# Sandwich layer on eight cores: eight weight slots and a reordered start for the first unit, scratch copies kept by five units

## The reference

```python
# x: (32, 2048, 1024) f32
x = x + layernorm(attn(layernorm(x)))
x = x + layernorm(ffn(layernorm(x)))

def attn(x):       # 16 heads of 64; segments of 512 tokens, every 4th token belongs to a head's set
    Q, K, V = x @ Wq + bq, x @ Wk + bk, x @ Wv + bv
    # head h takes, in each segment, the tokens with offset h % 4 (128 of them)
    scores = sum(Qs * Ks, over the 64 elements) * 64 ** -0.5
    attn = softmax(scores, over the 128 tokens)[..., None] * Vs
    # zero elsewhere
    return out @ Wo + bo

def ffn(x):        # integer weights, int32, times 1/127
    h = silu(x @ wg.T) * (x @ wu.T)      # hidden 3072
    return h @ wd.T
```

## Time and profile before

| | us |
|---|---|
| median of 3 runs | 2325.8 (2325.51 to 2326.94) |
| the profiled execution | 2324.59 |
| its span, slowest core | 2323.0 (the other cores 2317.4 to 2322.8) |
| PE busy | 2232.1 (96%) |
| DVE, ACT, POOL busy | 987.4, 645.4, 233.5 |
| mean granted clock of PE | 0.99 |

### The profile page before, as it was taken

One profiled execution on the slowest core, in us unless ns is written; L12 is line 12 of the kernel. 1 busy time (PEld: TensorE's weight loads), 2 busy tenths in 40 slices (PEclk: granted clock), 3 DMA queues, 4 the chain that ended last, 5 costly groups with the idle time before them and its releaser, 6 DMA issues.

```text
span 2323.0 us, 31558 instructions; the slowest of 8 cores (2317.4 to 2323.0 us)
## 1 busy us (share of the span) xinstructions
PE 2232.1 (96%) x10193; PEld 1017.1 (44%) x10400; DVE 987.4 (43%) x1697; ACT 645.4 (28%) x848; POOL 233.5 (10%) x633
## 2 busy tenths in 40 slices
PE   4789989999999999999999999999999999999997
PEld 2334434444444444444444444444444444444443
DVE  3552352534525344352544525344362544435222
ACT  3313213232231322313232231322323232231311
POOL 4211111010100101001010100101001010100100
PEclk9899999999999999999999999999999999999999
DMA  9696876764435444455544445355543534434340
GB/s 197 104 172 150 166 188 129 215 137 151 145 110 183 107 148 129 139 157 134 180 105 155 134 124 171 96 171 139 151 145 109 173 109 155 127 118 145 90 146 37
DMA packets 201953, 327.74 MB, mean 141 GB/s; under 512 B 127936, under 2 KB 127936, under 8 KB 201792
## 3 DMA queue, kind: packets, MB, share of 16 engines
q1 hardware_dynamic: 70272, 255.88, 34.0%
q0 software_dynamic: 12672, 39.85, 10.9%
q10 hardware_dynamic: 118848, 29.98, 7.1%
HBM read 290.01 MB, written 46.14 MB: 145 GB/s over the span
## 4 chain that ended last, share of the span: by engine, by line
PE 90%; DMA 6%; issue 1%; ACT 1%; ACTq 1%; DVE 1%; SPq 0%; POOL 0%; POOLq 0%; DVEq 0%
PE pf L479 27%; PE pf L475 27%; PE pf L493 26%; PE pa L401 7%; PE pa L450 2%; DMA gu<-wgu 2%; DMA x<-x 2%; DMA scr_gu<-gu 1%; ACTq L775 1%; ACT xh L752 0%; DMA xT<-xh 0%; PE pt L395 0%; PE pf L401 0%; PE pa L438 0%; DMA gu<-scr_gu 0%
## 5 line engine op out<-in xcount | busy, mean ns | idle before, releaser
L475 PE MATMUL pf<-xT,gu 128*128 128x512 bf16 x3010 | 724.8, 381 | 21.9 <-DMA gu<-wgu 12.6
L479 PE MATMUL pf<-xT,gu 128*128 128x512 bf16 x3012 | 722.4, 380 | 3.3 <-issue 0.2
L493 PE MATMUL pf<-wd_sb,h 128*128 128x512 bf16 x3009 | 662.8, 379 | 3.3
L632 DVE TENSOR_TENSOR h<-silu,pf 128x512 bf16<-128x512 bf16 x384 | 264.0, 687 | 795.8 <-PE pf L479 642.9
L802 ACT ACTIVATE silu<-pf 128x512 bf16<-128x512 f32 x384 | 228.8, 596 | 973.9 <-PE pf L475 950.4
L475 PEld LDWEIGHTS pf<-xT,gu 128*128 128x128 bf16 x3072 | 300.9, 98 | 385.6 <-issue 27.7
L479 PEld LDWEIGHTS pf<-xT,gu 128*128 128x128 bf16 x3072 | 301.6, 98 | 365.6 <-issue 5.7
L493 PEld LDWEIGHTS pf<-wd_sb,h 128*128 128x128 bf16 x3072 | 300.3, 98 | 361.6
L281 POOL TENSOR_SCALAR stats<-stats 128x1 f32<-128x1 f32 (+1 forms) x124 | 29.9, 241 | 1829.6 <-DVE stats L563 1825.7
L642 DVE TENSOR_TENSOR x<-y,x 128x1024 f32<-128x1024 f32 x64 | 78.3, 1223 | 301.1 <-ACT y L815 301.1
L401 PE MATMUL pa<-xT,wqkv_sb 128*128 128x512 bf16 x722 | 167.0, 383 | 6.3 <-DMA xT<-xh 2.3
(11 more groups left out here) (43 smaller groups left out, 685.2 us busy)
## 6 DMA issues: line engine op xcount, KB each, us to landing
gu<-scr_gu SPq DMA_DIRECT2D x336, 512.0 KB, 3.6
x<-x SPq DMA_DIRECT2D x64, 512.0 KB, 5.8
out<-x SPq DMA_DIRECT2D x64, 512.0 KB, 2.7
gu<-wgu POOLq DMA_DIRECT2D x48, 512.0 KB, 9.2
scr_gu<-gu SPq DMA_DIRECT2D x24, 512.0 KB, 8.7
wqkv_sb<-wqkv POOLq DMA_DIRECT2D x12, 512.0 KB, 11.6
wd_sb<-wd POOLq DMA_DIRECT2D x24, 256.0 KB, 30.3
wo_sb<-wo POOLq DMA_DIRECT2D x4, 512.0 KB, 16.0
```

Source lines behind the costliest of these rows:

```text
L475: ins = eng.matmul(g[:], gu[:, o:o + 128], half(xT3, kc), start=(kc == 0), stop=(kc == KC - 1))
L479: ins = eng.matmul(u[:], gu[:, o:o + 128], half(xT3, kc), start=(kc == 0), stop=(kc == KC - 1))
L493: ins = eng.matmul(pf[m % 4][:], h[:, 512 * kc + 128 * j:512 * kc + 128 * j + 128], wd[:, D * kc + 512 * hf:D * kc + 512 * hf + 512], star ...
L632: eng.tensor_mul(half(h, k), half(silu, k % 2), pf[2 * (k % 2) + 1][:]).then_inc(v_h, 1)
```

## The change

Five things are changed.

1. The first unit has a ring of eight slots. Four more (`gux`) lie where the third x buffer `x[2]` lies, which unit 2 is the first to use. From unit 1 on there are four again (`slot`, `gu_slot`, `before`).
2. At the start x of unit 0 is loaded alone. The projection weights wait for its third row and are issued between the rows' `l1` steps, unit 1's x waits for the query weights, and the twelve first down loads come after the gate/up loads. Stores of unit 0's chunks wait until 18 chunks are done; unit 2's x waits for the end of unit 0's gate/up stage and for the last four stores.
3. DVE, ACT and PE have another order in the first unit: unit 1's `ln1` rows stand between the attention steps of unit 0, q of both halves comes before k, `out_proj(0)` before unit 1's transposes, and some `x3_apply` and evictions are swapped. In the tail of unit 0, `ln4(0, 0)` and `fin(0, 0)` stand before the `ln1` rows of unit 2.
4. PE waits for the identity alone, and ACT loads its table with a small exponential ahead of the first row.
5. `kept(k)` spreads the stores: unit 0 keeps 16 to 23, unit 1 keeps 0, 5, 10, 15, unit 2 keeps 1, 6, 11, 12, unit 3 keeps 2, 7, 8, 13, and unit 4 keeps 3, 4, 9, 14. A chunk is cast in each unit up to the one that keeps it: 24, 16, 12, 8 and 4 casting loads instead of 24, 16 and 8.

```diff
-        x = [E(nc.sbuf_tensor(f"x{i}", [128, 4 * D], F32)) for i in range(3)]
+        x = [E(nc.sbuf_tensor(f"x{i}", [128, 4 * D], F32)) for i in range(2)]
+        with contextlib.ExitStack() as pctx:
+            gux = pctx.enter_context(nc.sbuf_tensor("gux", [128, RING * 2 * D], BF16))
+        with contextlib.ExitStack() as pctx:
+            x.append(pctx.enter_context(nc.sbuf_tensor("x2", [128, 4 * D], F32)))
...
+        def kept(k):
+            return 0 if k >= 16 else 1 + (k - k // 4) % 4
         def cast(n):
-            return n % HCN < HCN - 8 * (n // HCN)
+            return n // HCN <= kept(n % HCN)
         def keeps(n):
-            return cast(n) and n % HCN >= HCN - 8 * (n // HCN + 1)
+            return n // HCN == kept(n % HCN)
+        def slot(n):
+            return n % (2 * RING) if n < HCN else n % RING
...
# SP
-                for u in range(2):
+                for j in range(4):
+                    load_x(0, j)
+                if units > 1:
+                    eng.wait_ge(d_q[0], 16)
                     for j in range(4):
-                        load_x(u, j)
+                        load_x(1, j)
+                eng.wait_ge(t_gu, 18)
                 for k in range(16, HCN):
-                    if k == 20 and units > 2:
-                        for j in range(4):
-                            load_x(2, j)
-                    keep_gu(0, k)
+                    keep_gu(k)
+                if units > 2:
+                    eng.wait_ge(t_gu, HCN)
+                    for j in range(4):
+                        eng.wait_ge(d_st[RING + j], 16)
+                        load_x(2, j)
...
# POOL
-                load_attn(0)
-                for k in range(RING):
-                    load_gu(0, k)
                 eng.wait_ge(v_one, 1)
-                for j in range(4):
-                    l1(0, j, 1)
-                    load_wd(2 * j)
-                    load_wd(2 * j + 1)
+                l1(0, 0, 1)
+                eng.wait_ge(d_x[0][2], 16)
+                for j in range(3):
+                    load_proj(0, j)
+                    l1(0, j + 1, 1)
+                load_wo(0)
+                for k in range(2 * RING):
+                    load_gu(k)
                 if units > 1:
                     for j in range(4):
                         l1(1, j, 1)
-                        for k in range(8 + 3 * j, 11 + 3 * j):
-                            load_wd(k)
+                for k in range(12):
+                    load_wd(k)
...
-                for k in range(RING, HCN):
-                    load_gu(0, k)
-                    if k == 15 and units > 1:
+                for k in range(2 * RING, HCN):
+                    load_gu(k)
+                    if k >= 12:
+                        load_wd(k)
+                    if k == 19 and units > 1:
                         l2(1, 0, 4)
-                    if k in (14, 16, 18, 20):
-                        load_wd(13 + k // 2)
...
# ACT
+                eng.wait_ge(v_one, 1)
+                eng.activation(st(IDLE, 4), st(HALF, 4), AF.Exp)
...
                     q_evict(1, 0)
                     q_evict(1, 1)
+                x3_apply(0, 0)
+                if units > 1:
                     v_evict(1, 0)
+                x3_apply(0, 1)
+                if units > 1:
                     v_evict(1, 1)
-                for j in range(4):
-                    x3_apply(0, j)
-                    turn_evict(0, 1, j)
+                turn_evict(0, 1, 0)
+                turn_evict(0, 1, 1)
+                x3_apply(0, 2)
+                turn_evict(0, 1, 2)
+                x3_apply(0, 3)
+                turn_evict(0, 1, 3)
```

More of the change, by code:

```diff
@@ L187, in landed, with scratch @@
         def landed(n):
-            return sum(1 for m in range(n % RING, n + 1, RING) if cast(m) == cast(n))
+            return sum(1 for m in range(n + 1) if slot(m) == slot(n) and cast(m) == cast(n))
         def stores(n):
-            return sum(1 for m in range(n % RING, n + 1, RING) if keeps(m))
+            return sum(1 for m in range(n + 1) if slot(m) == slot(n) and keeps(m))
+        def scratch(n):
+            m = HCN * kept(n % HCN) + n % HCN
+            return d_st[slot(m)], 16 * stores(m)
         def xh_slot(j):
@@ L508, in _ @@
                 proj_v(0, 1)
+                for j in range(4):
+                    out_proj(0, j)
                 if units > 1:
@@ L724, in _ @@
                             ln1(a + 1, j)
-                    for j in range(3):
+                    for j in range(0 if p else 1, 3):
                         ln4(p, j)
@@ L840, in _ @@
                 if units > 1:
[L841 to L842 removed]
+                    for j in range(4):
+                        x1_apply(1, j)
                     for j in range(4):
```

119 lines of the change are left out of this document (64 added, 55 removed).

## The result

The changed kernel takes 2299.6 us (median of three runs, 2298.4 to 2301.6) where the kernel before takes 2326.0 us (median of four): the ratio is 0.9887, with a 95% interval of 0.9868 to 0.9907. Forecast were 2295.0 us in a range of 2284 to 2309, so the direction was right, and the gain of 26.4 us is 3.2 us (a ninth) smaller than the 29.6 us of the sum. In a later session the same kernel took 2299.4 us.

What follows compares the result with a forecast made beforehand. The kernel was taken as bound by matmuls wherever they are fed, so only PE's losses could be won. Terms -8.9 - 11.8 - 0.5 - 9.4 + 1.0 = -29.6 us, from 2324.6 to 2295.0 us; range 2284 to 2309.

Steps and rivals of the forecast that it cites:

- x alone and first: Start: x of unit 0 lands sooner with casting loads behind it; projections start at 22.2 us, -6.0 us.
- Unit 1's rows between unit 0's vector work: Start, on DVE: each row holds back only what comes after it; output projection at 46.0 instead of 55.74 us.
- The check that I named, the scores waiting for over 3 us: Start: forecast wrong there if the scores still wait for a unit 1 row by more than 3 us.
- Output projection before the transposes: Start, on PE: output projection ahead of unit 1's transposes; first gate matmul at 78.0 us, -8.9 us, ends 74 and 83.
- rival 1: Start bound by delivery: x no faster, unit 1's rows at 47 us, first gate matmul at 83; 2300 us, chance 0.12.
- Eight slots, stores held back: Unit 0's gate/up stage: no load waits for a store; 88.7 us, -11.8 us, ends 87 and 96.
- The sign that I named, no wait for gate/up weights in unit 0: Unit 0's gate/up stage: PE never waits for gate/up weights, stage under 90 us.
- Down of unit 0: Unit 0's down stage: scaled rows ready since POOL no longer stands in loads waiting for stores; -0.5 us.
- Scratch kept by five units: Unit 1's gate/up stage: fewer stores, 3 us lost instead of 12.4, -9.4 us; units 2 to 4 cast more, +1.0 us.
- Rival 2: Feed stays short: unit 0 keeps 7 us of stalls, unit 1 keeps 9 us; 2308 us, chance 0.15.
- Rival 3: Units 2 to 4: 18 casting loads each miss by 3.6 us, losing 65 us; 2359 us, chance 0.03.
- Rival 4: All goes well: POOL's issues hide, unit 1 loses nothing, first gate matmul at 74; 2286 us, chance 0.08.

Runs made afterwards that it cites:

- stores not held back: The changed kernel without the wait that holds unit 0's stores until 18 chunks are done; 2307.8 us, ratio 0.9907 to the kernel before.
- x not alone: The changed kernel with all loads at the start asked for together as before, unit 1's x right behind unit 0's; 2302.0 us, ratio 0.9905 to the kernel before.
- rows late: The changed kernel with unit 1's four statistics later on DVE and four down loads between POOL's `l1` steps; 2297.8 us, ratio 0.9867 to the kernel before.

## Why the prediction was right, and where it was off

- **x alone and first** (-6.0 for the projections): -5.1 from slowest core to slowest core (28.16 to 23.06), -4.8 on the medians. POOL was last, as said: its three weight issues start at 11.28, 14.07 and 16.70 us. The x queue alone was faster than my 251 GB/s on this core (below), which changed nothing. The price of 2.0 us plus bytes over 436 GB/s, which I held against the trace, is given in the Trainium skill ("DMA: Bandwidth & Descriptors", section on the anatomy of one DMA) for transfers that GpSimd issues. Here x goes by SP's queue, so the trace does not speak against that price.
- **Unit 1's rows between unit 0's vector work** (output projection at 46.0): this is the step that failed; it came at 50.30. The term had the first row 2.0 + 5.4 us after its request. Requested at 18.1 us, it was taken at 29.93: 11.8 us instead of 7.4, and the third at 41.10 instead of 36.7. Between those two the rows took 4.8 and 6.4 us, near my 5.4, so the term that was too small is the first landing among casting loads just issued. The same step has a second mistake: I let each row "hold back only what comes after it" and then costed only the fourth one, while the third stood before a softmax half whose scores were ready. The check that I named, the scores waiting for over 3 us, looked at the wrong place: they waited 2.6 us at most, while the delay came one step later, at the third row before the second softmax half.
- **Output projection before the transposes** (first gate at 78.0): the step itself held. From the output projection's start to the first gate matmul I had 32.0 us, measured are 32.5 (50.30 to 82.81). Taken back, it costs 4.0 us. The late start was passed on in full, 4.3 us. This is rival 1's number on this core (83), and its time of 2300 us is nearer to the measured 2299.6 than the forecast's 2295.0. Of its mechanism one half came true, unit 1's rows as late as 47 us (46.19); the other, that x of unit 0 gets no faster, did not.
- **Eight slots, stores held back** (-11.8): -12.05, and 90.09 us on the slowest core for the 88.7 forecast. That the term came out so close is in part luck: the hold-back that I took for free carries 5.75 us of it, which the sum does not have. (By my own figures the room was 24.8 us, 166.7 less 2.9 less 139, not 22.) The sign that I named, no wait for gate/up weights in unit 0, held but for one wait: PE stood 0.7 us for a `gux` load on core 2.
- **Down of unit 0** (-0.5): 0. It was core 0's alone; the other cores had 43.2 us before and have it now. Unit 2's x is asked for at 177.65 us (forecast 172 to 183), and costs nothing.
- **Scratch kept by five units** (-9.4 and +1.0): -7.85 and +0.15. The stage takes 99.93 us (100.1 forecast), with 2.2 us of waits on core 2, one of them the named scratch load of chunk 16. The gain is smaller since core 0's 109.52 us was 2.6 us over the median of the cores. DMA's share from 271 to 291 us fell from 1.04 to 0.84.
- **Rival 2** (2308 us): not here, but "stores not held back" is this rival's mechanism, with 2307.8 us on a chip where the kernel before takes 2329.3. **Rival 3** (casting loads late in units 2 to 4): unit 2 takes 97.12 us. **Rival 4** (2286 us): it needed the rows early and unit 1 free of loss; with the rows moved and ACT reordered 2294 us were reached, and unit 1 still lost 2.2 us.

Against the medians of the cores the sum misses by 2.4 us at the start and 1.55 us in unit 1, both less gain than forecast, and the rest nearly cancels. In unit 1 the miss comes with the core the term was read on, the slowest before, whose stage was 2.6 us over the median of the cores. In the start it is the late rows; single cores differ there by 4 us.

Left open: what of unit 1's last 2 us goes when the store leaves the scratch loads' way, why unit 1 takes 2 us more in "x not alone" and "rows late", and the small stalls of unit 3 (0.3 us on the slowest core, up to 0.6 on others). A fifth slot was not tried.

## What to carry to other kernels

On an engine that works in order, ask of each instruction that waits for data of the next unit what stands behind it, and do so for every one of them, not for the last alone: moving four such steps out of the softmax brought the first gate matmul 3.1 us forward here, and 2.4 us more once a few steps of the engines behind were moved too. The same holds for a queue: a store that waited for a casting load held up the load behind it for 5 us, with the DMA engines nearly idle for 3 of them. A transfer that nobody needs yet still takes its share of the DMA engines; one wait that held eight stores back was worth 5.75 us, and work moved into a stage that is short of transfers cost 10.3 us with few slots. Before a faster delivery is built, look whether its consumers can take it: at the first gate matmul x alone was worth nothing in one order and 4.5 us in the other.

## What the runs showed of the hardware

From 6 to 10 us, where only x of unit 0 moves, and then from 40 to 70 us, where casting loads fill the engines; and the 16 matmuls of the output projection in the changed kernel, and 15 of them in the kernel before:

```profile
6.00:10.00 4.00, 0.00 (x0) 0.00 (x0) 2.03 (x4) 0.00 (x0) 1.15 (x4) 1.00 0.97 303
40.00:70.00 30.00, 17.62 (x86) 7.89 (x86) 25.20 (x49) 12.28 (x13) 16.93 (x37) 0.77 1.05 177
50.30:55.75 5.45, 5.45 (x19) 2.13 (x20) 3.84 (x6) 0.82 (x1) 5.45 (x12) 0.66 1.05 177
55.74:59.70 3.96, 3.96 (x15) 1.35 (x14) 3.22 (x6) 0.96 (x2) 0.00 (x0) 0.90 1.05 173
```

A plain copy ran at 303 GB/s with the engines at 0.97 on core 2 (an estimate of 312 for full engines, near the 318 that I had worked out from a share of 0.79), and at 247 to 300 GB/s on the other cores; with casting loads 171 to 177 GB/s are written. The other thing is the half clock: after 9.45 us of idle, the output projection's 16 matmuls took 5.45 us (0.34 each, granted clock 0.66), against 3.96 us for 15 before (0.26 each, 0.90), where PE had transposed right ahead of them. A stall before short work costs more than its own length; I had 4.7 us for these sixteen.
